# A head's operand loads moved ahead of its predecessor's denominators, and its q and k rows loaded by 6 transfers in place of 12, in a 16-head attention kernel

## The chip, the cores and the metric

The kernel runs on one core of one Trainium2 chip. The metric is the device time of one execution in microseconds (us). Engines are named as in the profile: PE is the matrix engine (PEld its weight loads), DVE the vector engine, ACT the scalar engine, POOL the general-purpose engine, SP the engine that here does nothing but wait on semaphores and start DMA transfers ("SPq" in the profile's rows). Transfers are carried out by 16 DMA engines that the core has.

## The reference

One transformer layer on x of shape (4, 1024, 128), in float32: layer norm, attention with 16 heads of 8 dimensions and a bias that depends only on the distance between query and key, a gate, then a layer norm and a linear layer on values rounded to fp8. The part that matters here:

```python
proj = x @ w_in
k, v, q = jnp.split(proj, 3, axis=-1)          # heads: (b, 16, s, 8)
scores = jnp.einsum('bhqd,bhkd->bhqk', q, k) * scale
scores = scores + _tisa_bias(amplitudes, sharpness, offsets, s)[None]   # a Toeplitz matrix per head
weights = jax.nn.softmax(scores, axis=-1)
attn = jnp.einsum('bhqk,bhkd->bhqd', weights, v)
out = attn.transpose(0, 2, 1, 3).reshape(b, s, d)
gated = out @ w_gate + b_gate
```

## The kernel before, in words

**Setup** (0 to 70 us of the trace): layer norm, the products for q, k and v, and the bias vector of each head. q and k are split in a high and a low float16 part and stored to DRAM (`q_scratch`, `k_scratch`, `store_qk`, line 247); the bias vectors go to `g_scratch` (float32) and to `gh_scratch` and `gl_scratch` (float16 parts).

**Attention** (70 to 563 us) works on one head after another, in a hardware loop of 8 rounds with 2 heads each. A head has 8 groups (`GPH`), one for each 128 keys of every batch entry, and a group has 4 steps, one per batch entry. In a step PE makes 128 x 1024 scores (`scores`, line 869); for three steps of four DVE adds the bias from `t128` and writes them out (`add_bias`, line 938, the instruction is at L945); for the fourth PE adds the bias itself, by a product of `ident2` and `t64`. ACT exponentiates all four (L988, L996), and PE multiplies them with v (`products`, line 899). A ninth column of ones in v makes the softmax denominators, so they fall out of the same products. PE runs two groups ahead of the products with its scores (`LAG` = 2).

**Buffers of a head.** There are two sets: `qb`, `kb`, `t128`, `t64`, used in turn (p = 0, 1). A load fills one set (`load`, line 779): `load_qk` (line 233) brings q rows with 4 transfers and k rows with 8, each row block twice because the high and the low parts are multiplied crosswise; then `load_bias` (1 transfer of 960 KB), `load_bias_parts` (2 of 248 KB) and `load_maxima` (2 small ones). PE waits for all 17 of them before the first score of the head (`head_in`, line 875).

**Denominators of a head.** When the products of a head are complete, DVE and ACT copy them out of PSUM in the second group of the next head (`copy_half`, L736 and L737), and signal `o_ready`. SP then sends the denominators, 4 rows of 1024, to a 128 x 32 tile (`send_denominators`, L765). DVE takes their reciprocals after the additions of the fourth group (`RECIPROCAL` = 3, lines 966 to 975), in its own fixed order. SP stores the reciprocals (L790), waits until they are in DRAM, spreads them back over partitions (L771), waits for the multiplication on POOL (L857, L863), and stores the head's output (L796); that is `normalise_and_store`.

**Order of the work around the change.** Everything is written out by hand. Each engine runs its list in order and stops at a wait. SP's list is the loop from line 815 on. DVE's part of it that matters:

```python
for g in range(2 * GPH):
    for b in range(DPG):
        add_bias(i, g, b)
    ...
    if g == GPH + RECIPROCAL:
        eng.wait_ge(den_in[0], i * 16 + 16)
        eng.reciprocal(dc[0][:, :], dc[0][:, :]).then_inc(inv_ready[0], 1)
```

`z_ready` counts DVE's additions and `sp_ready` the fourth steps that PE has finished, so the two together say that a head's bias and q and k rows have been read for the last time. `groups_done` counts finished groups of products and starts at `SETS` = 4.

Of the kernel before, what the change touches and what calls it, by code (L numbers as in the profile page):

```python
# [22 lines left out]
F16 = mybir.dt.float16  # L23
# [8 lines left out]
H, KB = 16, 21  # L32
HD = D // H
P = 128
NTOK = B * S
# [27 lines left out]
def attention_block(nc, io, out):  # L63
    with ExitStack() as ctx:
# [6 lines left out]
        def dram(name, shape, dt):  # L71
            return nc.dram_tensor(name, shape, dt, kind="Internal").ap()


        q_dram = dram("q_scratch", [2, P, 2, B, HALF], F16)
        k_dram = dram("k_scratch", [2, P, NTOK], F16)
        g_dram = dram("g_scratch", [32, GN], F32)
        gh_dram = dram("gh_scratch", [32, GN], F16)
        gl_dram = dram("gl_scratch", [32, GN], F16)
# [134 lines left out]
        def cols(b):  # L214
            return slice(b * S, (b + 1) * S)
# [16 lines left out]

        def load_qk(eng, h, p, done):

            for c in range(2):
                for rep in range(2):
                    r = ROW * c + 16 * rep
                    eng.dma_start(qb[p][r:r + 16, :],  # L238
                                  q_dram.rearrange("a (h d) c b n -> c h a d (b n)", d=HD)[c, h]).then_inc(done, 16)
            for c in range(2):  # L240
                for hl in range(2):
                    for rep in range(2):
                        r = ROW * c + 16 * hl + 8 * rep
                        eng.dma_start(kb[p][r:r + 8, :],  # L244
                                      k_dram.rearrange("a (h d) n -> h a d n", d=HD)[h, hl]).then_inc(done, 16)

        def store_qk(eng, b, done):

            for ready, part, hl in ((qh_ready, 0, 0), (kh_ready, 2, 0), (ql_ready, 1, 1), (kl_ready, 3, 1)):
                eng.wait_ge(ready, b + 1)  # L250
                src = split[:, part, cols(b)]
                if part < 2:
                    eng.dma_start(q_dram[hl, :, :, b, :], src.rearrange("p (c n) -> p c n", n=HALF))\
                       .then_inc(done, 16)
                else:
                    eng.dma_start(k_dram[hl, :, cols(b)], src).then_inc(done, 16)

        def load_maxima(eng, h, p, done):
            for c in range(2):
                eng.dma_start(qb[p][ROW * c + 32:ROW * c + 33, :],  # L260
                              m_dram[h, :].rearrange("(o b c n) -> c o b n", o=1, c=2, n=HALF)[c]).then_inc(done, 16)
        LOADS = 17
        QK_LOADS = 12
        LOADS_G = 13

        def copy_v(eng, h, p):

# [21 lines left out]
        with nc.Block() as block:  # L289
            @block.sync  # L290
            def _(eng):
# [37 lines left out]
                load_bias(eng, 0, 0, head_in[0])  # L329
                load_bias_parts(eng, 0, 0, head_in[0])  # L330

                for ready, part, dst, rows in ((qh_ready, 0, qb[0], (0, 16)), (ql_ready, 1, qb[0], (8, 24)),
                                               (kh_ready, 2, kb[0], (0, 8)), (kl_ready, 3, kb[0], (16, 24))):
                    eng.wait_ge(ready, B)
                    for c in range(2):
                        src = split[0:HD, part, :]
                        if part < 2:
                            src = src.rearrange("p (b c n) -> p c b n", c=2, n=HALF)[:, c]
                        for r in rows:
                            eng.dma_start(dst[ROW * c + r:ROW * c + r + HD, :], src).then_inc(first_in, 16)  # L340
# [398 lines left out]
        def settled(eng, s, value):  # L739


            eng.wait_ge(s, value)
            eng.sem_inc(queue_steps, 1)
# [30 lines left out]
        with nc.Block() as block:  # L774
            @block.sync
            def _(eng):
                def load(h, p):
                    h = in_range(h)
                    load_qk(eng, h, p, head_in[p])
                    load_bias(eng, h, p, head_in[p])  # L780
                    load_bias_parts(eng, h, p, head_in[p])
                    load_maxima(eng, h, p, head_in[p])
# [29 lines left out]
                eng.sem_inc(queue_steps, 1)  # L812
                with eng.Fori(0, NH2) as i:

                    settled(eng, groups_done, i * (2 * GPH) + SETS)
                    with eng.If(i > 0):
                        settled(eng, o_ready[0], i * 2 + 1)
                        settled(eng, o_ready[1], i * 2 + 1)
                        send_denominators(eng, 1)
                    load(i * 2 + 1, 1)  # L820
                    with eng.If(i > 0):
                        normalise_and_store(i * 2 - 1, 1, i - 1)

                    settled(eng, groups_done, i * (2 * GPH) + (GPH + SETS))
                    settled(eng, o_ready[0], i * 2 + 2)
                    settled(eng, o_ready[1], i * 2 + 2)
                    send_denominators(eng, 0)
                    with eng.If(i < NH2 - 1):
                        load(i * 2 + 2, 0)
                    with eng.If(i > NH2 - 2):  # L830

                        eng.wait_ge(vst_in, H)
                        eng.wait_ge(o_stored[0], 16 * B * NH2)
                        eng.wait_ge(o_stored[1], 16 * B * NH2)
                        for b in range(B):
                            eng.dma_start(num[b][0:EARLY, :], o_dram[b, 0:H - 2]).then_inc(num_in[b], 16)
                    normalise_and_store(i * 2, 0, i)
# [676 lines left out]
```

## Time and profile before

| | us |
|---|---|
| median of 3 runs | 629.25 (627.89 to 629.95) |
| the profiled execution | 628.96 |
| span of its trace | 627.1 |
| PE, DVE, ACT busy | 571.8, 558.1, 551.1 |
| POOL busy | 101.7 |
| DMA traffic | 53.82 MB |

The span is what the trace covers from its first to its last instruction; the 1.9 us between it and the execution's own time lie around it. PE, DVE and ACT are each busy for 88 to 91% of the span. Granted clock of the profiled execution: 0.955 of full speed on average.

### The profile page before, as it was taken

The page shows a single profiled execution, that of the slowest core. Times are in us where ns is not written, and L with a number is a line of the kernel's source. Part 1 is how long each engine was busy: PE and PEld are TensorE (multiplying, and loading weights), DVE is VectorE, ACT ScalarE, POOL GpSimd, SP SyncE. Part 2 cuts the span into 40 slices and gives each one's busy share as a digit, 9 for nine tenths or more (in the row PEclk, how much of TensorE's full clock was granted, in tenths as well). Part 3 has the DMA queues.
Part 4 walks back from the last instruction along what each step waited for, and adds up shares of the span by engine and source line. Part 5 has one row for each costly group of instructions (what it writes and reads, how often), then busy time and mean ns, then how long its engine had stood idle before and what let it go on. Part 6 is the DMA issues. An engine that isn't in the chain of part 4 may idle for free.

```text
span 627.1 us, 12678 instructions
## 1 busy us (share of the span) xinstructions
PE 571.8 (91%) x3987; PEld 155.6 (25%) x3987; DVE 558.1 (89%) x686; ACT 551.1 (88%) x610; POOL 101.7 (16%) x96
## 2 busy tenths in 40 slices
PE   5794399999999999999999899999999999999945
PEld 2442022222222222222222122222222222225532
DVE  6975499999999999999999899999999999974885
ACT  2853399999999999999999999999999999983474
POOL 5731510010101010101010101010101100012630
PEclk8797599999999999999999999999999999999957
DMA  9127642516161616161617161616252434410004
GB/s 234 52 49 194 156 106 45 146 22 137 28 139 26 144 25 142 24 141 29 135 30 133 27 140 37 128 42 126 48 121 65 100 69 96 128 26 9 1 0 135
DMA packets 29819, 53.82 MB, mean 86 GB/s; under 512 B 9461, under 2 KB 20986, under 8 KB 28666
## 3 DMA queue, kind: packets, MB, share of 16 engines
q1 hardware_dynamic: 28954, 53.02, 37.4%
q10 hardware_dynamic: 848, 0.59, 0.3%
q8 instruction: 8, 0.13, 0.1%
q14 instruction: 9, 0.07, 0.0%
HBM read 43.27 MB, written 9.16 MB: 84 GB/s over the span
## 4 chain that ended last, share of the span: by engine, by line
ACT 38%; issue 31%; DVE 7%; DMA 7%; SPq 7%; PE 7%; POOL 1%; ACTq 1%; DVEq 0%; POOLq 0%
ACT pbuf L988 16%; ACT split L988 15%; ACT pbuf L996 3%; DVE pbuf L459 3%; PE ps L1188 3%; ACT split L996 2%; DMA qb<-m_scratch 2%; SPq L340 2%; DMA r_scratch<-dc 2%; PE ps L1232 1%; SPq L238 1%; DMA kb<-split 1%; ACT o_sbs L737 1%; SPq L244 1%; DMA x_sb<-in_L_attn_x 1%
## 5 line engine op out<-in xcount | busy, mean ns | idle before, releaser
L945 DVE TENSOR_TENSOR pbuf<-ps,t 128x1024 f32<-128x1024 f32 x192 | 229.9, 1216 | 21.6 <-PE ps L886 17.5
L945 DVE TENSOR_TENSOR split<-ps,t 128x1024 f32<-128x1024 f32 x192 | 231.3, 1222 | 12.0 <-PE ps L886 6.3
L988 ACT ACTIVATE pbuf<-pbuf 128x1024 f32<-128x1024 f32 x192 | 203.2, 1211 | 21.1 <-DVE pbuf L945 20.9
L886 PE MATMUL ps<-qb,kb 64*128 64x512 f16 x1024 | 183.6, 389 | 23.8 <-SPq L801 15.0
L988 ACT ACTIVATE split<-split 128x1024 f32<-128x1024 f32 x192 | 199.3, 1220 | 0.1
L911 PE MATMUL ps<-split,vst 128*32 128x512 f32 x1024 | 136.0, 604 | 1.0 <-ACT split L996 1.0
L911 PE MATMUL ps<-pbuf,vst 128*32 128x512 f32 x1024 | 136.4, 605 | 0.0
L886 PEld LDWEIGHTS ps<-qb,kb 64*128 64x128 f16 x1024 | 48.5, 92 | 309.6 <-DVE pbuf L945 115.1
L895 PE MATMUL ps<-t64s,ident 128*64 128x512 f16 x512 | 80.1, 393 | 0.0
L996 ACT ACTIVATE split<-ps 128x1024 f32<-128x1024 f32 x64 | 75.7, 1183 | 0.0
L996 ACT ACTIVATE pbuf<-ps 128x1024 f32<-128x1024 f32 x64 | 75.0, 1173 | 0.0
L863 POOL TENSOR_TENSOR o_sbs<-o_sbs,rd 128x1024 f32<-128x1024 f32 x8 | 19.1, 2387 | 196.3 <-DMA rd<-r_scratch 196.3
L857 POOL TENSOR_TENSOR o_sbs<-o_sbs,rd 128x1024 f32<-128x1024 f32 x7 | 16.7, 2385 | 186.0 <-DMA rd<-r_scratch 186.0
L911 PEld LDWEIGHTS ps<-split,vst 128*32 128x32 f32 x1024 | 20.3, 108 | 31.5 <-issue 29.7
L911 PEld LDWEIGHTS ps<-pbuf,vst 128*32 128x32 f32 x1024 | 20.1, 108 | 29.0 <-issue 29.0
L895 PEld LDWEIGHTS ps<-t64s,ident 128*64 128x64 f16 x512 | 18.0, 108 | 31.0 <-issue 31.0
L459 DVE TENSOR_SCALAR pbuf<-x_sb,mv,st 128x128 f32<-128x128 f32 x32 | 18.4, 861 | 1.5 <-POOL st L362 1.5
L1188 PE MATMUL ps<-wgate,v_all 128*128 128x256 f32 x64 | 18.1, 405 | 0.0
L1270 ACT ACTIVATE pbuf<-ps 128x256 f32<-128x256 f32 x16 | 6.0, 381 | 13.3 <-PE ps L1188 13.3
L1122 POOL TENSOR_TENSOR x_sb<-x_sb,pbuf 128x256 f32<-128x256 f32 x16 | 11.5, 725 | 27.8 <-DVE pbuf L1387 27.8
L268 POOL COPY vst<-v_all 128x256 f32 (+1 forms) x16 | 6.4, 398 | 52.1 <-PE ps L911 48.1
L736 DVE COPY o_sbs<-ps 128x512 f32<-128x512 f32 x16 | 10.9, 680 | 3.5 <-PE ps L911 3.5
(144 smaller groups left out, 326.2 us busy)
## 6 DMA issues: line engine op xcount, KB each, us to landing
t<-g_scratch SPq DMA_DIRECT2D x16, 960.0 KB
kb<-k_scratch SPq DMA_DIRECT2D x120, 64.0 KB
t64s<-gh_scratch SPq DMA_DIRECT2D x16, 248.0 KB
t64s<-gl_scratch SPq DMA_DIRECT2D x16, 248.0 KB
qb<-q_scratch SPq DMA_DIRECT2D x60, 64.0 KB
x_sb<-in_L_attn_x SPq DMA_DIRECT2D x4, 512.0 KB, 6.7
q_scratch<-split SPq DMA_DIRECT2D x8, 256.0 KB, 3.3
k_scratch<-split SPq DMA_DIRECT2D x8, 256.0 KB, 3.6
```

Of the source, the lines that this page charges most:

```text
L340: eng.dma_start(dst[ROW * c + r:ROW * c + r + HD, :], src).then_inc(first_in, 16)
L459: last = eng.tensor_scalar(xn[:, n, :], x_sb[:, n, :], mv[:, n, 0:1], st[:, 0, n:n + 1], ALU.subtract, ALU.mult)
L857: eng.tensor_tensor(o_sb[1], o_sb[1], rd[:, :], ALU.mult).then_inc(o_norm, 1)
L863: eng.tensor_tensor(o_sb[0], o_sb[0], rd[:, :], ALU.mult).then_inc(o_norm, 1)
L886: last = eng.matmul(ps[:, u + c, :], kb[p][rows, keys], qb[p][rows, b * HALF:(b + 1) * HALF], start=True, stop=True)
L895: last = eng.matmul(ps[64 * m:64 * m + 64, u + c, :], ident2[:, :], t64[p][:, c0:c0 + HALF], start=False, stop=True, skip_group_check=True)
L911: last = eng.matmul(ps[32 * b:32 * b + 32, 6 + c, :], vst[p][:, b * TB + t, :], slot(g, b)[:, c * HALF:(c + 1) * HALF], start=(t == 0), st ...
L945: eng.tensor_tensor(slot(g, b), banks(unit(k), 2), t128[p][:, t * P:t * P + S], ALU.add).then_inc(z_ready, 1)
L988: eng.activation(buf, buf, ACT.Exp).then_inc(p_ready, 1)
L996: eng.activation(buf, banks(4, 2), ACT.Exp).then_inc(p_ready, 1)
L1122: eng.tensor_tensor(xs, xs, gate[:, j % NG, :], ALU.add).then_inc(x1_ready, 1)
L1188: last = eng.matmul(ps[:, j % 4, m * 2 * D:(m + 1) * 2 * D], num[n // TB][:, (n % TB) * P:(n % TB + 1) * P], wgate[:, :], start=False, sto ...
```

## The change

A head's load no longer waits for the products of the head that used the buffers before. It waits for `z_ready` and `sp_ready`, and stands ahead of `send_denominators` in SP's list, at both places of the loop. `load_qk` brings q rows with 4 transfers and k rows with 2. Each of the six reads its DRAM rows twice by a leading dimension of step 0 and size 2. For that `k_scratch` is laid out by head, and the order of the rows in `qb` and `kb` changes: q is now high, high, low, low and k high, low, high, low, where it was the other way round. The counts of the semaphores follow (11 transfers a head, not 17). The transfers that fill head 0 in the setup keep their number and size.

```diff
-        k_dram = dram("k_scratch", [2, P, NTOK], F16)
+        k_dram = dram("k_scratch", [H, 2, HD, NTOK], F16)
...
         def load_qk(eng, h, p, done):
 
-            for c in range(2):
-                for rep in range(2):
-                    r = ROW * c + 16 * rep
-                    eng.dma_start(qb[p][r:r + 16, :],
-                                  q_dram.rearrange("a (h d) c b n -> c h a d (b n)", d=HD)[c, h]).then_inc(done, 16)
+            def repeated(v):
+                return bass.AP(tensor=v.tensor, offset=v.offset, ap=[[0, 2]] + [list(a) for a in v.ap])
+
             for c in range(2):
                 for hl in range(2):
-                    for rep in range(2):
-                        r = ROW * c + 16 * hl + 8 * rep
-                        eng.dma_start(kb[p][r:r + 8, :],
-                                      k_dram.rearrange("a (h d) n -> h a d n", d=HD)[h, hl]).then_inc(done, 16)
+                    r = ROW * c + 16 * hl
+                    eng.dma_start(qb[p][r:r + 16, :],
+                                  repeated(q_dram.rearrange("a (h d) c b n -> c a h d (b n)", d=HD)[c, hl, h]))\
+                       .then_inc(done, 16)
+            for c in range(2):
+                eng.dma_start(kb[p][ROW * c:ROW * c + 32, :],
+                              repeated(k_dram.rearrange("h a d n -> h (a d) n")[h])).then_inc(done, 16)
...
-        LOADS = 17
-        QK_LOADS = 12
-        LOADS_G = 13
+        LOADS = 11
+        QK_LOADS = 6
+        LOADS_G = 7
...
                 with eng.Fori(0, NH2) as i:
 
-                    settled(eng, groups_done, i * (2 * GPH) + SETS)
                     with eng.If(i > 0):
+                        settled(eng, z_ready, i * (2 * DPH))
+                        settled(eng, sp_ready, i * (2 * GPH))
+                    load(i * 2 + 1, 1)
+                    with eng.If(i > 0):
+                        settled(eng, groups_done, i * (2 * GPH) + SETS)
                         settled(eng, o_ready[0], i * 2 + 1)
                         settled(eng, o_ready[1], i * 2 + 1)
                         send_denominators(eng, 1)
-                    load(i * 2 + 1, 1)
-                    with eng.If(i > 0):
                         normalise_and_store(i * 2 - 1, 1, i - 1)
 
+                    with eng.If(i < NH2 - 1):
+                        settled(eng, z_ready, i * (2 * DPH) + DPH)
+                        settled(eng, sp_ready, i * (2 * GPH) + GPH)
+                        load(i * 2 + 2, 0)
                     settled(eng, groups_done, i * (2 * GPH) + (GPH + SETS))
                     settled(eng, o_ready[0], i * 2 + 2)
                     settled(eng, o_ready[1], i * 2 + 2)
                     send_denominators(eng, 0)
-                    with eng.If(i < NH2 - 1):
-                        load(i * 2 + 2, 0)
```

SP's list at the start of a loop round, before the change. Rows without a tile set registers or branch; sizes are those of the destination.

```order
L816 COMPARE_AND_BRANCH [waits groups_done]
L742 ISA
L765 DMA dc1<-o_sbs 128x1x32 [waits o_ready0,o_ready1]
L816 UNCONDITIONAL_BRANCH
L238 ISA
L238 DMA qb1<-q_scratch 16x1x2048 x2
L238 ISA
L238 DMA qb1<-q_scratch 16x1x2048 x2
L244 DMA kb1<-k_scratch 8x4096 x2
L244 ISA
L244 DMA kb1<-k_scratch 8x4096 x6
```

The same place with the change:

```order
L816 COMPARE_AND_BRANCH
L743 REGISTER_ALU
L743 REGISTER_ALU [waits z_ready]
L816 UNCONDITIONAL_BRANCH [waits sp_ready]
L241 ISA
L241 DMA qb1<-q_scratch 16x1x2048
...
L241 DMA qb1<-q_scratch 16x1x2048
L245 ISA
L245 DMA kb1<-k_scratch 32x1x4096 x2
```

The wait for `groups_done` and `o_ready` and the transfer of the denominators are gone from here, and eight transfers of 8 rows have become two of 32 rows.

SP's list where the load ends, before the change:

```order
L227 DMA t128_1<-g_scratch 128x1920
L230 REGISTER_ALU
L230 DMA t64s<-gh_scratch 64x1984
L231 DMA t64s<-gl_scratch 64x1984
L260 ISA
L260 DMA qb1<-m_scratch 1x4x512
L260 ISA
L260 DMA qb1<-m_scratch 1x4x512
L821 COMPARE_AND_BRANCH
L790 DMA r_scratch<-dc1 128x32 [waits inv_ready1]
```

And with the change:

```order
L227 DMA t128_1<-g_scratch 128x1920
L230 REGISTER_ALU
L230 DMA t64s<-gh_scratch 64x1984
L231 DMA t64s<-gl_scratch 64x1984
L261 ISA
L261 DMA qb1<-m_scratch 1x4x512
L261 ISA
L261 DMA qb1<-m_scratch 1x4x512
L820 COMPARE_AND_BRANCH
L743 ISA
L766 DMA dc1<-o_sbs 128x1x32 [waits groups_done,o_ready0,o_ready1]
L791 DMA r_scratch<-dc1 128x32 [waits inv_ready1]
```

The transfer of the denominators now stands behind all eleven transfers of the load, directly ahead of the one that needs DVE's reciprocals of it.

## Rows read from the trace of the kernel before

**Rows 1.** The page: busy time, then busy tenths of PE in 40 slices.
```profile
PE 571.8 (91%) x3987; PEld 155.6 (25%) x3987; DVE 558.1 (89%) x686; ACT 551.1 (88%) x610; POOL 101.7 (16%) x96
PE   5794399999999999999999899999999999999945
```

**Rows 2.** Waits, 85 to 560 us: total us, times, longest.
```profile
DVE pbuf L945 <- PE ps L886: 2.4, 4, 1.9
PE ps L886 <- DMA qb<-m_scratch: 2.0, 2, 1.8
```

**Rows 3.** Timeline of SP: start us, us, what. One head's sequence, then others.
```profile
110.02 2.97 SPq L238 DMA_DIRECT2D qb<-q_scratch  x4
...
128.23 1.30 SPq L771 DMA_DIRECT2D rd<-r_scratch  x4
...
446.33 0.65 SPq L765 DMA_DIRECT2D dc<-o_sbs  x1
447.22 2.99 SPq L238 DMA_DIRECT2D qb<-q_scratch  x4
450.31 3.06 SPq L244 DMA_DIRECT2D kb<-k_scratch  x8
453.55 0.36 SPq L227 DMA_DIRECT2D t<-g_scratch  x1
...
457.18 0.35 SPq L790 DMA_DIRECT2D r_scratch<-dc  x1
466.83 1.30 SPq L771 DMA_DIRECT2D rd<-r_scratch  x4
473.02 1.81 SPq L796 DMA_DIRECT2D o_scratch<-o_sbs  x4
...
545.83 0.35 SPq L790 DMA_DIRECT2D r_scratch<-dc  x1
547.98 1.28 SPq L771 DMA_DIRECT2D rd<-r_scratch  x4
```

**Rows 4.** Timeline of DVE, the first four groups of the same head.
```profile
438.51 4.96 DVE L945 TENSOR_TENSOR pbuf<-ps,t 128x1024 f32<-128x1024 f32 x4
443.39 0.68 DVE L736 COPY o_sbs<-ps 128x512 f32<-128x512 f32 x1
...
453.93 0.34 DVE L971 RECIPROCAL dc<-dc 128x32 f32<-128x32 f32 x1
```

**Rows 5.** The line that sends denominators: count, durations ns, first and last start us.
```profile
L765 SPq DMA_DIRECT2D dc<-o_sbs x15: 635/641/648, 109.1 to 537.5; - x15
```

**Rows 6.** Windows of 1 us; the last columns are granted clock, DMA share, GB/s.
```profile
450.00:451.00 1.00, 1.00 (x10) 0.16 (x8) 0.76 (x1) 1.00 (x2) 0.00 (x0) 1.00 0.12 49
451.00:452.00 1.00, 1.00 (x14) 0.25 (x10) 1.00 (x2) 1.00 (x2) 0.00 (x0) 1.00 0.60 143
...
458.00:459.00 1.00, 1.00 (x14) 0.24 (x10) 0.99 (x2) 1.00 (x3) 0.00 (x0) 1.00 0.99 240
...
463.00:464.00 1.00, 1.00 (x12) 0.19 (x4) 0.94 (x1) 1.00 (x2) 0.00 (x0) 1.00 0.19 64
464.00:465.00 1.00, 1.00 (x8) 0.24 (x6) 0.96 (x1) 1.00 (x2) 0.00 (x0) 1.00 0.12 47
```

**Rows 7.** Waits of SP over the whole span: total us, times, longest.
```profile
SPq L743 <- DMA r_scratch<-dc: 138.4, 15, 12.0
```

**Rows 8.** Windows around PE's idle stretch in the setup, and the restart after it.
```profile
57.00:60.00 3.00, 0.00 (x0) 0.00 (x0) 0.00 (x0) 0.00 (x0) 0.00 (x0) 0.50 0.51 72
...
73.00:76.00 3.00, 2.83 (x12) 0.39 (x8) 2.50 (x3) 2.85 (x3) 2.88 (x3) 0.50 1.03 350
76.00:79.00 3.00, 2.18 (x18) 0.58 (x18) 3.00 (x3) 2.99 (x4) 2.94 (x2) 0.97 0.82 248
```

**Rows 9.** SP's timeline, the first load of the loop.
```profile
82.12 3.12 SPq L238 DMA_DIRECT2D qb<-q_scratch  x4
```

**Rows 10.** Timeline of all engines where one load came late: idle before, and releaser.
```profile
346.78 0.39 PE L886 MATMUL ps<-qb,kb 64*128 64x512 f16 x2 [1.83 <-DMA qb<-m_scratch]
```

More of the change, by code:

```diff
@@ L255, in store_qk @@
                 else:
-                    eng.dma_start(k_dram[hl, :, cols(b)], src).then_inc(done, 16)
+                    eng.dma_start(k_dram[:, hl, :, cols(b)], src).then_inc(done, 16)
         def load_maxima(eng, h, p, done):
@@ L330, in _ @@
                 load_bias_parts(eng, 0, 0, head_in[0])
-                for ready, part, dst, rows in ((qh_ready, 0, qb[0], (0, 16)), (ql_ready, 1, qb[0], (8, 24)),
-                                               (kh_ready, 2, kb[0], (0, 8)), (kl_ready, 3, kb[0], (16, 24))):
+                for ready, part, dst, rows in ((qh_ready, 0, qb[0], (0, 8)), (ql_ready, 1, qb[0], (16, 24)),
+                                               (kh_ready, 2, kb[0], (0, 16)), (kl_ready, 3, kb[0], (8, 24))):
                     eng.wait_ge(ready, B)
```

## The prediction

> **What bounds the kernel now.** I read the page first, then the waits of the attention stretch, then SP's and DVE's timelines over one head, then the DMA share in windows of 1 us. The page shows PE, DVE and ACT busy at nine tenths or more from slice 6 to slice 38 [rows 1]. No wait of substance stands there: DVE waited 2.4 us in all for PE, and PE 2.0 us in all for a load that was late, 1.8 us of it at one head [rows 2, 10]. So the most that earlier loads can win is about 2 us. The heads follow each other at a steady pace: the denominators are sent 15 times, first at 109.06 (row: 109.1) and last at 537.54 (row: 537.5), so a head takes 428.4 / 14 = 30.6 us [rows 5].
>
> The question is then what the new order can cost. I take one head as the model and count from Z, the end of a head's last addition. In the trace the four additions that begin the next head start at 438.51, so Z = 438.5 [rows 4]. The denominators leave at 446.33, which is Z + 7.8; the load's transfers start at 447.22 [rows 3]; DVE comes to the reciprocal at 453.93, which is Z + 15.4, and finds them there [rows 4]. From the end of the reciprocal to the next Z are 30.6 - 15.4 - 0.3 = 14.9 us of additions that follow it in DVE's list.
>
> **How long a load takes.** Behind the load SP starts the small transfer to `r_scratch` at 457.18 and goes on only at 466.83, when it has landed: 9.65 us for 16 KB [rows 3]. The last such transfer, the only one with no load ahead of it, takes 545.83 to 547.98, 2.15 us [rows 3]. All 15 together cost SP 138.4 us [rows 7]. So a transfer waits for the data of those started before it. From the load's first transfer to that landing are 466.83 - 447.22 = 19.6 us; at an earlier head 128.23 - 110.02 = 18.2 [rows 3].
>
> What sets the 19.6 us? At 450 to 451 only q rows move: the DMA share is 0.12, which is two engines of 16, at 49 GB/s, so 24.5 GB/s each [rows 6]. A q transfer reads 2 x 8 rows, its outermost dimension having size 2. When the k transfers of 8 rows come, the share goes to 0.60; while the bias rows move it is 0.99 at 240 GB/s, 15 GB/s for an engine [rows 6]. At 464 to 465 it is back at 0.12 and 47 GB/s: fourteen engines have finished and two still carry the rest [rows 6]. I read this so: the two engines that carry all q rows are the last to finish, and their bytes set the length of a load.
>
> **The change, part by part.**
>
> 1. *k rows in 2 transfers.* Each reads 256 KB through a source whose outermost dimension is the added one, of size 2, as in the q transfers. I expect two engines again, and the same two, since four q transfers in flight together gave no more than a share of 0.12. Before, each carried an eighth of 8 x 64 KB, 64 KB in all; now half of 512 KB, 256 KB. The extra 192 KB (197,000 B) take 8.0 us at 24.5 GB/s, or 13.1 us at the contended 15 GB/s [rows 6]. I take 8.0, since the other fourteen will long have finished. If the k rows spread as before, it is nothing: the lower end.
>
> [...]
>
> 2. *Six transfers fewer to start.* Eight k transfers take 450.31 to 453.55 on SP, 3.24 us [rows 3]; two at the pace of the q transfers (3.09 us for 4, 0.77 each) take 1.5. That is 1.7 us less. It lets the bias rows start 1.7 us earlier, and I count it in full; at the other end it is worth nothing, where the two engines are never short of work.
>
> So a load and the transfer behind it take 19.6 + 8.0 - 1.7 = 25.9 us.
>
> 3. *Load at Z.* The load now waits for the additions and for PE's fourth step, and starts at Z + 0.5 (0.5 for two waits, a branch and registers: denominators to first q transfer took 0.24 us beyond the first's own 0.65 [rows 3], and there are more of these now). SP must be free by then, see below.
>
> 4. *Denominators behind the load.* They are sent when the load's eleven transfers are started, about Z + 8.5, and land when its data have, at Z + 0.5 + 25.9 = Z + 26.4. DVE reaches the reciprocal at Z + 15.4 and must stop there, because the additions of groups five to eight stand behind it in its list. PE can make only two steps of scores ahead, and ACT gets nothing to exponentiate, so all three stop. The stall is 26.4 + 0.1 - 15.4 = 11.1 us. The cover that the denominators had before (7.6 us between their start and DVE's arrival) is gone.
>
> 5. *Restart.* [...] DVE lost about 1 us there: it was busy 2.50 of 3 us at 73 to 76, and half a us more may be lost before that [rows 8]. I take 1.0; ends 0 and 2.5 (half of 5 us, if PE paced all of it).
>
> Sum of one boundary: 11.1 + 1.0 = 12.1 us; the head takes 42.7 us, not 30.6. SP's other work fits: from the reciprocal at Z + 26.8, 2.2 us to `r_scratch`, then 466.83 to 474.83 for spreading, multiplying and storing, 8.0 us [rows 3], ends by Z + 38, before the next Z at 42.7. And the load has landed long before PE wants it, so the 2.0 us of [rows 2] go.
>
> Heads 0 to 13 have their denominators behind a load, 14 boundaries: 14 x 12.1 = 169.4. Head 1's load starts at 82.12 [rows 9] and now needs until about 107.5, while head 0's Z is 109.1 - 7.8 = 101.3; the load sent at that Z finds the two engines occupied for 4 us longer than it would start itself: + 4. Less the 2.0: 171.4. On the profiled execution's own 628.96 that gives 800.4; that execution lies 0.3 below the median of the runs shown (629.25). I say **800 us**. The layout of `k_scratch` and the new order of the rows change no count of rows or bytes, and the setup's transfers keep their shapes: nothing.
>
> **The rivals.**
>
> *A: the k rows cost no more than before.* If the data spread over engines as they did, a load takes 19.6 - 1.7 = 17.9; or, by the fastest head of [rows 3], 18.2 - 1.7 = 16.5. Denominators land at Z + 18.4: a stall of 3.1, and with a PE that barely cools 0.3 more: 14 x 3.4 - 2 = 46, 675 us. For it: one transfer with 32 destination rows could be cut along those. Against it: q's 16 destination rows did not help q.
>
> [...]
>
> *B: the denominators do not wait (faster or the same).* They are 4 rows, and if they went through engines that are not the two late ones they could land as soon as the bias rows of those have, about 463.3, where the share is down to 0.19 [rows 6], less 1.7 for the earlier start: 14.4 us after the load's first transfer, Z + 14.9. The point that decides is Z + 15.4: below it DVE never stops, the loads are in time, and the 2 us of [rows 2] are won: 627 us. For it: fourteen engines are idle at the end of a load. Against it: the `r_scratch` transfer waited for the last of the load at every head [rows 7], and it would need this margin of 0.5 us at each of 14 heads.
>
> *C: the two engines do worse.* If q and k rows share them at the contended rate throughout, the load takes 19.6 + 13.1 = 32.7, the stall is 17.9 and with 2.5 for the clock a boundary costs 20.4: 629 + 14 x 20.4 + 10 = 925 us. Against it: two engines alone moved 47 to 49 GB/s [rows 6].
>
> **How the numbers follow.** Forecast 0.78; A 0.12; B 0.04; C 0.06. The forecast's own spread comes from the load: the heads of the trace differ by 18.2 to 19.6 and more where a load was late; 22.5 to 29 us for a load make 12.1 into 8.7 to 15.2, so 629 + 14 x 8.7 = 751 to 629 + 14 x 15.2 + 7 = 849. I widen the low side to 740 for k rows that share less evenly. Range 740 to 850. About 0.3% (1.9 us) is what a measurement of this kernel can tell from no change. Faster by more than that 0.02 and within it 0.03 (both from B, and from a load that for some reason is short), slower 0.95.
>
> **What would show it.** In the changed trace DVE's reciprocals (L971 and L975 before) should stand behind an idle stretch of 8 to 14 us whose releaser is the transfer dc<-o_sbs, 14 times; starts of L765's successor about 42.7 us apart; the DMA share in windows of 1 us at 0.12 and some 50 GB/s for 8 us or more at the end of each load; the granted clock down to 0.50 once a head; q and k transfers 4 and 2 a head. Waits of DVE for the denominators under 2 us, or a share near 1 to the load's end, would make it wrong; so would stalls of the size of A with the two-engine tail absent.

## The result and the profile after

The changed kernel takes 782.2 us (median of 4 runs, 778.7 to 784.5) against 629.6: a ratio of 1.242, 95% interval 1.239 to 1.246. It is slower by 153 us. The forecast was 800 with a range of 740 to 850. The profiled execution took 778.7 us, its span is 776.8.

From the page of the changed kernel: busy time, busy tenths of PE in 40 slices, and the granted clock of PE in tenths. They answer to [rows 1].

```profile
PE 599.3 (77%) x3987; PEld 153.8 (20%) x3987; DVE 556.8 (72%) x686; ACT 558.6 (72%) x610; POOL 101.5 (13%) x96
PE   6872978959595968778695959595949687799965
PEclk7795889979798898979797979797978989799976
```

DVE and ACT do the same work as before, within 8 us, and PE is busy longer by 28 us, part of it at the lower clock (0.865 of full speed on average over the execution, 0.955 before). Their share of the span fell because they stand still once a head. The waits of the attention stretch (85 to 710 us) say for what; they answer to [rows 2].

```profile
ACT pbuf L993 <- DVE pbuf L950: 139.7, 43, 9.8
DVE dc L976 <- DMA dc<-o_sbs: 68.4, 7, 10.6
DVE dc L980 <- DMA dc<-o_sbs: 62.5, 7, 10.1
PE ps L891 <- DMA qb<-m_scratch: 5.7, 1, 5.7
```

DVE waited 130.9 us for the denominators in 14 stops: 3.4 us at the first, 9.2 to 10.6 at the others, 9.3 on average. It did not wait for them at all before. ACT waited for DVE in turn.

One head in SP's timeline, as in [rows 3]:

```profile
145.12 3.23 SPq L241 DMA_DIRECT2D qb<-q_scratch  x4
148.55 1.35 SPq L245 DMA_DIRECT2D kb<-k_scratch  x2
...
153.95 0.60 SPq L766 DMA_DIRECT2D dc<-o_sbs  x1
169.86 0.36 SPq L791 DMA_DIRECT2D r_scratch<-dc  x1
...
177.62 1.70 SPq L797 DMA_DIRECT2D o_scratch<-o_sbs  x4
185.89 3.38 SPq L241 DMA_DIRECT2D qb<-q_scratch  x4
```

and the same head in DVE's, as in [rows 4]:

```profile
144.71 4.96 DVE L950 TENSOR_TENSOR pbuf<-ps,t 128x1024 f32<-128x1024 f32 x4
...
169.42 0.35 DVE L976 RECIPROCAL dc<-dc 128x32 f32<-128x32 f32 x1 [9.21 <-DMA dc<-o_sbs]
169.69 3.42 DVE L950 TENSOR_TENSOR pbuf<-ps,t 128x1024 f32<-128x1024 f32 x3
173.60 1.22 DVE L950 TENSOR_TENSOR pbuf<-ps,t 128x1024 f32<-128x1024 f32 x1 [0.50 <-PE ps L891]
175.51 2.54 DVE L950 TENSOR_TENSOR pbuf<-ps,t 128x1024 f32<-128x1024 f32 x2 [0.69 <-PE ps L891]
```

Z is 144.7. The load starts 0.4 us later. The denominators are sent at 153.95, with the load's transfers started, and are there at 169.4: 24.3 us after the load's first transfer, Z + 24.7. Over the 14 heads with a load ahead of their denominators this takes 24.1 to 26.0 us, 24.8 on average. DVE stands from 160.2 on. After the reciprocal it loses 1.2 us more, waiting for PE.

Windows of the same head (the last three columns: granted clock, DMA share, GB/s; the first after the window is PE's busy time), as in [rows 6, 8]:

```profile
153.00:154.00 1.00, 1.00 (x14) 0.24 (x10) 1.00 (x2) 1.00 (x3) 0.00 (x0) 1.00 0.99 379
...
159.00:160.00 1.00, 1.00 (x11) 0.26 (x10) 1.00 (x1) 1.00 (x2) 0.00 (x0) 1.00 0.12 49
...
165.00:166.00 1.00, 0.00 (x0) 0.00 (x0) 0.00 (x0) 0.00 (x0) 0.00 (x0) 0.50 0.11 46
...
171.00:172.00 1.00, 1.00 (x6) 0.23 (x7) 1.00 (x2) 0.94 (x1) 0.00 (x0) 0.50 0.00 0
...
175.00:176.00 1.00, 1.00 (x14) 0.25 (x10) 0.49 (x1) 1.00 (x2) 1.00 (x1) 1.00 0.00 0
```

The share falls from 0.81 at 156 to 157 to 0.18 in the next window: fourteen engines have moved their part of the load by 157. From there to 168, eleven of the 24 us, two engines work alone at 46 to 57 GB/s and a share of 0.11 to 0.18. Two is read from the share (0.12 of 16 engines is 1.9); no view names the engines of a transfer. PE's clock is at half speed, 0.50, from 165 to 174 and back at 1.00 at 175.

The sending of denominators, the row that answers to [rows 5]:

```profile
L766 SPq DMA_DIRECT2D dc<-o_sbs x15: 593/599/612, 118.7 to 687.3; - x15
```

A head takes 568.6 / 14 = 40.6 us, 10.0 more than before (the first of the 14 steps 35.2, the other 13 on average 41.0), and the first denominators leave 9.7 us later. That is 140.1 + 9.7, and the spans differ by 149.7: all of the loss is in these two.

### The profile page after: what moved, and what is told of

It reads as the page before. It is cut to its first block, busy times and chain, and to the rows that moved or that the text cites. A ratio compares the mean times of both kernels' runs of the same rounds, so it can differ in the third digit from the quotient of the medians.

```text
span 776.8 us, 12583 instructions
## 1 busy us (share of the span) xinstructions
PE 599.3 (77%) x3987; PEld 153.8 (20%) x3987; DVE 556.8 (72%) x686; ACT 558.6 (72%) x610; POOL 101.5 (13%) x96
## 4 chain that ended last, share of the span: by engine, by line
DMA 30%; PE 28%; SPq 14%; issue 7%; DVE 6%; ACT 4%; POOL 1%; DVEq 0%; ACTq 0%; POOLq 0%
DMA dc<-o_sbs 28%; PE ps L916 12%; PE ps L891 8%; SPq L241 5%; PE ps L900 4%; DVE pbuf L950 3%; SPq L245 2%; SPq L261 2%; DMA qb<-m_scratch 2%; DVE split L950 2%; PE ps L1193 2%; ACT split L993 1%; SPq L230 1%; ACT pbuf L993 1%; PE ps L1237 1%
## 5 line engine op out<-in xcount | busy, mean ns | idle before, releaser
L993 ACT ACTIVATE pbuf<-pbuf 128x1024 f32<-128x1024 f32 x192 | 197.1, 1059 | 161.9 <-DVE pbuf L950 159.7
L891 PE MATMUL ps<-qb,kb 64*128 64x512 f16 x1024 | 191.8, 409 | 147.3 <-DVE pbuf L950 123.4
L993 ACT ACTIVATE split<-split 128x1024 f32<-128x1024 f32 x192 | 189.4, 1064 | 1.5 <-DVE split L950 1.4
L916 PE MATMUL ps<-split,vst 128*32 128x512 f32 x1024 | 146.0, 646 | 1.0 <-ACT split L1001 1.0
L891 PEld LDWEIGHTS ps<-qb,kb 64*128 64x128 f16 x1024 | 44.3, 94 | 438.3 <-DVE pbuf L950 234.5
L900 PE MATMUL ps<-t64s,ident 128*64 128x512 f16 x512 | 86.3, 420 | 0.0
L1001 ACT ACTIVATE split<-ps 128x1024 f32<-128x1024 f32 x64 | 65.8, 1028 | 0.0
L1001 ACT ACTIVATE pbuf<-ps 128x1024 f32<-128x1024 f32 x64 | 65.1, 1017 | 0.0
L976 DVE RECIPROCAL dc<-dc 128x32 f32<-128x32 f32 x7 | 2.5, 353 | 68.4 <-DMA dc<-o_sbs 68.4
L980 DVE RECIPROCAL dc<-dc 128x32 f32<-128x32 f32 x8 | 2.8, 352 | 62.5 <-DMA dc<-o_sbs 62.5
L916 PEld LDWEIGHTS ps<-split,vst 128*32 128x32 f32 x1024 | 21.0, 112 | 35.2 <-issue 27.6
```

The lines of the kernel that those rows point to most:

```text
L891: last = eng.matmul(ps[:, u + c, :], kb[p][rows, keys], qb[p][rows, b * HALF:(b + 1) * HALF], start=True, stop=True)
L900: last = eng.matmul(ps[64 * m:64 * m + 64, u + c, :], ident2[:, :], t64[p][:, c0:c0 + HALF], start=False, stop=True, skip_group_check=True)
L916: last = eng.matmul(ps[32 * b:32 * b + 32, 6 + c, :], vst[p][:, b * TB + t, :], slot(g, b)[:, c * HALF:(c + 1) * HALF], start=(t == 0), st ...
L993: eng.activation(buf, buf, ACT.Exp).then_inc(p_ready, 1)
L1001: eng.activation(buf, banks(4, 2), ACT.Exp).then_inc(p_ready, 1)
```

## The experiments

Twelve more kernels were run. Z is always the end of a head's last addition; "a head" is the time from one sending of denominators to the next, averaged over the 14 steps of the profiled execution. The length of a load is the time from its first transfer to the landing of the small transfer behind it (denominators or `r_scratch`); the rows show one head, and where a reading rests on the length, the average over 14 heads stands beside it.

| kernel | median, us | ratio to before (95%) | a head, us | DVE's wait for denominators a head |
|---|---|---|---|---|
| before | 628.4 to 629.6 | | 30.6 | 0 |
| the change | 782.2 | 1.239 to 1.246 | 40.6 | 9.3 |
| six transfers, order of before | 696.0 | 1.103 to 1.108 | 34.9 | 0 |
| order of the change, 12 transfers | 721.1 | 1.141 to 1.150 | 36.9 | 5.1 |
| change, denominators on another queue | 668.0 | 1.058 to 1.064 | 32.8 | 0 |
| change, rows interleaved | 630.0 | 1.000 to 1.004 | 30.4 | 0.2 |
| change, reciprocal two groups later | 699.6 | 1.109 to 1.114 | 35.1 | 3.7 |
| interleaved, order of before | 629.8 | 1.000 to 1.003 | 30.5 | 0 |
| interleaved, denominators on another queue | 631.0 | 1.002 to 1.005 | 30.5 | 0.1 |
| before, q by 8 rows | 629.0 | 1.000 to 1.003 | 30.5 | 0 |
| order of the change, q by 8 rows | 708.8 | 1.126 to 1.133 | 36.0 | 4.4 |
| the same, rows spread | 713.2 | 1.130 to 1.138 | 35.9 | 4.8 |
| before, q by 8 rows, rows spread | 629.6 | 1.000 to 1.003 | 30.5 | 0 |
| change, only k's dimensions exchanged | 672.2 | 1.062 to 1.077 | 33.6 | 2.9 |

### One half of the change at a time

**Six transfers, order of before.** The two loop pieces of SP stand as in the kernel before (the `-` lines of the diff's last part), all else as changed.

> The six transfers with the order of before (denominators ahead of the load). Theory (the two engines that carry q and k rows set a load's length, and the order decides who waits for it): the load takes about 24 us from its first transfer as in the changed kernel (145.12 to 169.4), starts at Z + 8.7 and lands at Z + 32.5, where PE wants it at Z + 29.1; no wait of DVE for denominators, but PE waits about 3.4 us a head for the load, 14 x 3.4 and some 5 us at head 1: 680 us (665 to 695). Rival (the k rows cost nothing, the order alone costs): 627 to 630 us.

Measured 696.0 us. The wait over 85 to 640 us, and the row of the line that sends the denominators:

```profile
PE ps L887 <- DMA qb<-m_scratch: 48.3, 15, 6.2
```
```profile
L766 SPq DMA_DIRECT2D dc<-o_sbs x15: 624/635/654, 120.6 to 609.7; - x15
```

No wait of DVE for denominators; PE waits for the load at every head, 42 us at 14 of them and 6.2 at head 1: 3.0 a head against 3.4 expected. The mechanism is as foretold. The time is 16 us over the 680 and 1 us above the range, because each stop costs 1.3 us beyond its own length (a head is 4.3 us longer) and the start loses 11.5 us, not 5. So the six transfers alone make the kernel slower.

**Order of the change, 12 transfers.** The kernel before with SP's two loop pieces from the change.

> The order of the change with the 12 q and k transfers of before. Theory: the denominators still land with the load's data, 19.6 us (18.2 to 22.5) after its first transfer, at Z + 20.1 against DVE's arrival at Z + 15.4: DVE stops for 4.7 us a head, with restart 5.3, so 14 x 5.3 - 2 = 72 us more: 701 us (680 to 720). Rival (only the bytes on two engines are at fault and an early load is good by itself): 627 to 630 us.

Measured 721.1 us, 1 us above the range expected. SP's timeline:

```profile
474.53 3.02 SPq L238 DMA_DIRECT2D qb<-q_scratch  x4
...
495.21 0.35 SPq L790 DMA_DIRECT2D r_scratch<-dc  x1
```

The load and what is behind it take 20.3 us (474.53 to 494.9, with 0.35 for the reciprocal taken off). DVE waits 5.1 us a head and a head grows by 6.3. So the new order is harmful with the old transfers too. The two halves alone cost 68 and 93 us, the whole change 153.

### Who holds the denominators back

**Denominators on another queue.** In the changed kernel POOL sends them, behind its `copy_v`:

```diff
@@ SP @@
-                        settled(eng, o_ready[0], i * 2 + 1)
-                        settled(eng, o_ready[1], i * 2 + 1)
-                        send_denominators(eng, 1)
@@ POOL @@
                     with eng.If(i > 0):
+                        settled(eng, o_ready[0], i * 2 + 1)
+                        settled(eng, o_ready[1], i * 2 + 1)
+                        send_denominators(eng, 1)
                         settled(eng, rd_in, i * (2 * 16 * B))
```

and the same for the other buffer.

> The changed kernel, but the denominators are sent by POOL, on its own queue, as soon as they are ready. Theory (a transfer waits for those started before it in its own queue, not for busy engines): they land within 3 us of their start, DVE's waits of 131 us for dc<-o_sbs go to under 10 us. What is left is SP's own cycle: load 24.2 us to its landing, then 8 us of spreading, multiplying and storing, 0.5 to the next load: 32.7 us a head, 2.1 above 30.6, so about 660 us (640 to 675). Rival (any small transfer waits while the two engines are occupied): no change, 775 to 790 us.

Measured 668.0 us, a head 32.8 us where 32.7 was worked out. The denominators' row and SP's timeline:

```profile
L766 POOL DMA_DIRECT2D dc<-o_sbs x15: 693/693/930, 118.8 to 577.6; - x15
```
```profile
452.13 0.36 SPq L791 DMA_DIRECT2D r_scratch<-dc  x1
467.13 1.30 SPq L772 DMA_DIRECT2D rd<-r_scratch  x4
```

The load still takes 24 us (443.0 to 467.1 here), but DVE waits 0.4 us in the whole execution. This late head does not test the queue, though: SP is behind by then, its load starts at 443.0, and POOL sends the denominators at 444.2, when the load has hardly begun. The second head does test it. Its rows from the timelines of SP, POOL and DVE:

```profile
141.59 3.25 SPq L241 DMA_DIRECT2D qb<-q_scratch  x4
...
149.25 0.70 POOL L766 DMA_DIRECT2D dc<-o_sbs  x1 [1.45 <-ACT o_sbs L738]
...
156.58 0.34 DVE L976 RECIPROCAL dc<-dc 128x32 f32<-128x32 f32 x1
...
165.78 1.30 SPq L772 DMA_DIRECT2D rd<-r_scratch  x4
```

All transfers of the load are started when POOL sends the denominators, DVE takes them without a stop 15.0 us after the load's first transfer, and the load lands at 24.2 us. So the denominators need not wait for the load once they are out of SP's queue. That it is the queue and not the engines is not shown: no row here tells which DMA engines carry a transfer that POOL sends, and they may be others than those of SP's. Nor is the way quite free. At the third head the denominators took 7.9 us to land, against 3.4 in the median of all.

The next thing in SP's queue, the store to `r_scratch`, now waits in their place, 15 us, and with it SP's cycle of load, spreading and storing. So the loads come late and PE waits for them, 12 times and 28.6 us in all. That the head came out at the 32.7 us worked out is partly luck: the first three steps take 30.5 us, the other eleven 33.4.

**Reciprocal later.** One constant, `RECIPROCAL = 5` in place of 3.

> The changed kernel with the reciprocal two groups later in DVE's list (RECIPROCAL 5, not 3). Theory (DVE stops only for what is left of the load when it arrives): DVE arrives at Z + 22.9, the denominators land at Z + 24.7 if SP starts the load at Z. But SP's storing now ends 9.9 us after the reciprocal, at Z + 33.2, 2.5 us after the next Z, so the load starts and lands 2.5 us later: a stall of 3.9 us a head (9.3 before), with restart 4.3, 14 x 4.3 + 6 = 66 us above the kernel before: 694 us (675 to 710). Rival (the time goes with the later start of anything behind the load, whatever DVE does): within 10 us of the changed kernel's 782.

Measured 699.6 us; DVE waits 52.1 us in all (the row: total, times), 3.7 a head against 3.9 expected:

```profile
  DMA dc<-o_sbs: 52.1, 13
```

DVE's fixed place for the reciprocal is the point that decides, as the prediction used it. SP's cycle takes back part of what a later place wins: at the head whose Z is 213.9 the load starts only at 216.7.

### What makes the load long

**Rows interleaved.** The same six transfers and bytes, but each source begins with its rows. For k the doubling moves inside. For q the inner dimension is now the high and the low part, and each of the two transfers brings both once. q and k rows are put in the order that fits, in the setup too.

```diff
             def repeated(v):
-                return bass.AP(tensor=v.tensor, offset=v.offset, ap=[[0, 2]] + [list(a) for a in v.ap])
+                rows, row = [list(a) for a in v.ap]
+                return bass.AP(tensor=v.tensor, offset=v.offset, ap=[rows, [0, 2], row])
...
-                for hl in range(2):
-                    r = ROW * c + 16 * hl
+                for a in range(2):
+                    r = ROW * c + 16 * a
                     eng.dma_start(qb[p][r:r + 16, :],
-                                  repeated(q_dram.rearrange("a (h d) c b n -> c a h d (b n)", d=HD)[c, hl, h]))\
+                                  q_dram.rearrange("a (h d) c b n -> c h d a (b n)", d=HD)[c, h])\
                        .then_inc(done, 16)
```

> The changed kernel with the same 6 transfers and the same bytes, but the rows interleaved, so that the source's outermost dimension has size 16 for k (each row doubled in the second dimension) and 8 for q. Theory (the outermost dimension sets the number of engines): no stretch at a DMA share of 0.12, a load lands about 14 to 15 us after its first transfer, the denominators at Z + 15 to 16, DVE stops for 0 to 1 us a head: 632 us (625 to 650). Rival (the doubled reading itself is slow, or the engines are chosen otherwise): as the changed kernel, 750 to 790 us.

Measured 630.0 us, 152 us less than the change; what differs is the order of the source's dimensions and the order of the rows that goes with it.

SP's timeline, then windows of 1 us as above:

```profile
442.38 3.27 SPq L242 DMA_DIRECT2D qb<-q_scratch  x4
...
458.08 0.36 SPq L792 DMA_DIRECT2D r_scratch<-dc  x1
```
```profile
452.00:453.00 1.00, 0.71 (x6) 0.24 (x6) 1.00 (x2) 1.00 (x2) 0.00 (x0) 1.00 1.18 353
...
456.00:457.00 1.00, 1.00 (x10) 0.32 (x8) 0.91 (x2) 1.00 (x2) 0.00 (x0) 1.00 0.14 24
```

The denominators are there 15.3 us after the load's first transfer (no head has them later than 15.9), and the load ends without the tail of two engines that took eleven us in the change: from 454 to 457 the share goes 0.76, 0.39, 0.14, and then it is 0.00.

**Only k's dimensions exchanged.** The changed kernel, with the k source as above and q as it is.

> The changed kernel with the two dimensions of the k source exchanged: 16 rows outermost, the doubling inside. The q transfers stay as they are. Heads 1 to 15 then multiply k rows with other q rows than they should, so the attention's values differ; the work is the same. Theory (each term by itself: k's 192 KB on the two engines made the load long, q's 128 KB on them are left): the load takes 16.5 to 18 us and not 24.2, the denominators land at Z + 17 to 18.5 against Z + 15.4, DVE stops for 1.5 to 3 us a head: 655 us (640 to 675). Rival (the doubled read or the size of 256 KB is at fault, not the dimension's place): 770 to 790 us.

Measured 672.2 us. SP's timeline, and the total and number of DVE's waits for the denominators:

```profile
472.20 3.21 SPq L241 DMA_DIRECT2D qb<-q_scratch  x4
...
490.57 0.36 SPq L793 DMA_DIRECT2D r_scratch<-dc  x1
```
```profile
  DMA dc<-o_sbs: 40.5, 14
```

The load takes 17.9 us (17.8 on average) and DVE waits 2.9 a head, both inside what was expected. So of the 24.3 us, 6.4 are k's bytes on two engines (7.0 on the averages), and that alone is 110 of the 153 us lost; the rest goes when q's dimensions are exchanged too (15.3 us to the landing, above).

### Are the two engines all of it?

In the kernel before, by the prediction's reading, q's two-engine transfers set the load's length. **q by 8 rows** tests it:

```diff
-                    r = ROW * c + 16 * rep
-                    eng.dma_start(qb[p][r:r + 16, :],
-                                  q_dram.rearrange("a (h d) c b n -> c h a d (b n)", d=HD)[c, h]).then_inc(done, 16)
+                    for hl in range(2):
+                        r = ROW * c + 16 * rep + 8 * hl
+                        eng.dma_start(qb[p][r:r + 8, :],
+                                      q_dram.rearrange("a (h d) c b n -> c h a d (b n)", d=HD)[c, h, hl]).then_inc(done, 16)
```

> The kernel before with one thing changed: each q transfer of 2 x 8 rows is split into two of 8 rows, 16 q and k transfers a head; order, setup stores and row order of before. Theory (q's two-engine transfers set the load's length in the kernel before too): the load to the landing behind it takes about 15 us instead of 19.6, the tail at a DMA share of 0.12 is gone, PE's 2.0 us of waits for loads go, nothing else changes: 627 us (625 to 629), at best 0.3% below before. Rival: four transfers more cost as much as they win, 629 us or more.

Measured 629.0 us, not to be told from before, and the reason given was wrong for the most part. The landing hardly moved (SP's timeline, then windows):

```profile
446.55 3.19 SPq L239 DMA_DIRECT2D qb<-q_scratch  x8
...
466.28 1.30 SPq L772 DMA_DIRECT2D rd<-r_scratch  x4
```
```profile
456.00:457.00 1.00, 1.00 (x10) 0.26 (x8) 0.94 (x2) 1.00 (x2) 0.00 (x0) 1.00 1.18 127
457.00:458.00 1.00, 1.00 (x10) 0.16 (x8) 1.00 (x2) 1.00 (x2) 0.00 (x0) 1.00 0.86 92
```

It comes 19.7 us after the first transfer, where the model head of the kernel before had 19.6. Over 14 heads the averages are 19.6 here and 20.5 before, so doing without the two engines was worth about 1 us. The tail of two engines is gone (the share is 0.56 at 463 to 464, 0.38 at 464 to 465, then 0.00), but for some four us in the middle, 455 to 459, the engines are busy at a share of 0.84 to 1.20 and move only 92 to 127 GB/s, where the kernel before had 240 at a share of 0.99 [rows 6].

**The same in the new order.**

> The same 8-row transfers with the early load of the change and the denominators behind it. Theory: the load is short again, so the denominators land at about Z + 15 to 16 against DVE's Z + 15.4, DVE stops for 0 to 1 us a head: 630 us (626 to 640), as with interleaved rows. The number of transfers (20 here, 11 in the change) does not matter. Rival (the number of transfers ahead of the denominators matters): 20 transfers start over about 10 us, so the denominators leave 2 to 3 us later than with 11 and 650 us or more result.

Measured 708.8 us: this expectation failed. A load was not short (19.5 us on average), and DVE waited 62.0 us in all, 4.4 a head. The rival's bound of 650 us was passed, but not for its reason: in the head traced the denominators left 10.1 us after the load's first transfer, where they left after 8.8 in the change, and landed 9.7 us after that. Transfers of eight rows, without a two-engine one among them, are not enough. What the runs show is the slow stretch, 92 to 127 GB/s at a share of 0.84 to 1.20 in the kernel before with q by 8 rows. That it comes from writing each transfer's rows to eight neighbouring partitions was a guess of mine, which no run shows; theory P below is that guess, and the numbers of engines named with theory E are assumed too. **Rows spread** sends the same transfers to every fourth of 32 partitions (`kb[p][r:r + 29:4, :]` for `kb[p][r:r + 8, :]`, likewise for `qb`, with the row order made to fit).

> The kernel with the early load and 8-row transfers that gave 708.8 us, with one thing changed: the 8 rows of a q or k transfer go to every fourth partition, over 32, and not to 8 adjacent ones. Same number of transfers, same bytes, same engines. Theory P (many engines that write into few neighbouring partitions hold each other up, and the bias rows behind them in the same queues): the load becomes as short as with interleaved rows, about 15 us, and the time 630 us (626 to 640). Theory E (what counts is that k rows use 8 engines and not 16, or that there are 20 transfers): no change, 700 to 715 us.

Measured 713.2 us, which is what theory E said, but the trace shows that the test did not isolate what it was to isolate:

```profile
470.86 6.25 SPq L239 DMA_DIRECT2D qb<-q_scratch  x8
...
487.13 0.61 SPq L766 DMA_DIRECT2D dc<-o_sbs  x1
490.95 0.34 SPq L791 DMA_DIRECT2D r_scratch<-dc  x1
```

A transfer to stepped partitions took SP 0.78 us to start, not 0.40, so the load's transfers needed 15.8 us and the denominators were sent 16.3 us after the first; they landed 3.4 us later. Here SP's starting is most of the landing's 19.7 us. **The same with the order of before:**

> The same spread rows with the order of before (denominators first). Theory P: the landing behind a load comes 15 us after its first transfer and not 19.7; PE waits for no load; 628 us (626 to 630), since there are only about 2 us to win. Theory E: 19.7 us to the landing and 628 to 630 us; the time does not tell them apart here, the landing does.

Measured 629.6 us, and the landing 19.9 us after the first transfer. By its own rule that would speak for theory E, but this test has the same fault as the one before it:

```profile
447.52 6.24 SPq L239 DMA_DIRECT2D qb<-q_scratch  x8
...
463.68 0.35 SPq L791 DMA_DIRECT2D r_scratch<-dc  x1
467.39 1.30 SPq L772 DMA_DIRECT2D rd<-r_scratch  x4
```

SP needed 16.2 us of the 19.9 to start what stands ahead of the small transfer. The landing decides between the theories as little as the time does. The row of the bias phase:

```profile
462.00:463.00 1.00, 1.00 (x10) 0.10 (x2) 1.00 (x2) 1.00 (x2) 0.00 (x0) 1.00 1.12 453
```

At the same DMA share as the slow stretch above the engines now move 453 GB/s. That fits theory P, but in this kernel the k rows were over before the bias rows began, so it does not prove it. The place of the rows, the overlap with the bias rows and the number of engines stay unseparated.

### Is there anything to win?

**Interleaved, order of before.** The interleaved kernel with SP's loop as before.

> Interleaved rows in 6 transfers, order of before (denominators ahead of the load). Theory: a load lands about 15 us after its first transfer instead of 19.6, so PE never waits for it (2.0 us in the kernel before) and DVE never for denominators (2.8 us in the interleaved kernel with the early load): 626 us, 2 below before (624 to 628.5). Rival (fuller use of the engines slows the three busy engines in another way): 630 us or more.

Measured 629.8 us, ratio 1.0003 to 1.0027, above the 624 to 628.5 expected. The load takes 13.5 us at this head, the shortest of 14; the average is 15.5, near the 15 expected:

```profile
447.67 3.22 SPq L242 DMA_DIRECT2D qb<-q_scratch  x4
...
461.15 1.30 SPq L773 DMA_DIRECT2D rd<-r_scratch  x4
```

PE no longer waits for a load, and a head takes 30.5 us, 1.8 less over 14 heads as forecast. But in its trace the first denominators leave at 111.5, 2.4 us later than in the profile of before, and the end is no earlier. Part of that may be chance: the kernel before with q by 8 rows has the setup of before, and its first leave at 110.4. Part is in the setup (a store to the new layout of `k_scratch` takes SP 0.6 us, not 0.35, in two places; its first scores start at 72.1, not 70.8); the shares were not separated.

**Interleaved, denominators on another queue.**

> Interleaved rows, the early load of the change, and denominators sent by POOL on its own queue. Theory: no engine waits for a load or for denominators; SP's cycle (load 15, then 8 to 10 of storing) is below 30.6 us: 626 us (624 to 628.5), equal to the interleaved kernel in the order of before. Rival (an early load or POOL's own sending costs something by itself): 2 us or more above that.

Measured 631.0 us, 1.002 to 1.005. DVE waits 0.8 us in all and PE for no load, and the time is no better; the 626 us expected of both kernels did not come. The trace is of the fastest of its 12 executions (629.0 us; the slowest took 634.0), so it does not show what the median has beyond it. No version beat the kernel before. Of the versions with the order of the change, only those with interleaved rows came within 0.5% of it.

## Why the prediction was right

The forecast's mechanism is what happened, and the time was 18 us below the 800, inside the range. The profiled execution grew by 149.7 us where the sum has 171.4. Its stops were shorter (130.9 us in all, not 155.4) and its restarts cheaper (9.2, not 14), while the start cost more (9.7, not 4), and the 2.0 taken off at the end are already in the head's 40.6. Step by step:

*What bounds it, and the 2 us to win.* Right. The kernels without any late load gained those 2 us in the loop and no more.

*A transfer waits for those ahead of it.* Right for the denominators in SP's queue, at every head of the changed kernel: they landed 24.1 to 26.0 us after the load's first transfer. Denominators that POOL sent in the middle of a load did not wait for its end (15.0 us against 24.2 at the second head), so the rule is not one for any small transfer; whether queue or engines make the difference stayed open.

*Part 1, k rows on two engines, 8.0 us.* The mechanism is shown: two engines alone, at a share of 0.12, and 6.4 us of load length by exchanging k's dimensions alone (24.3 to 17.9 us). The place of one dimension decides here; rival A fell. The size is not: see part 2. The 192 KB behind the 8.0 take it that k's eight-row transfers ran on eight engines, these two among them. No run shows that number: the share was 0.60 when the k rows came [rows 6], and 0.30 to 0.31 while q moved by 8 rows (447 to 450, in the kernel before with q by 8 rows). What the runs show in the term's place is the 6.4 us (7.0 on the averages).

*Part 2 and the length of a load, 25.9.* Measured 24.3 at the head shown, 24.8 on average. This is the term that was mis-sized. Parts 1 and 2 together add 6.3 us (8.0 - 1.7) to a load; from the average of the kernel before, 20.5, to that of the change it was 4.3. The model head's 19.6 lies below that average (18.2 to 22.5), so the forecast came closer than its reasoning: the low base hid part of the error, by luck. The sum added k's bytes to the 19.6 us of before as if nothing else in them changed. But the 19.6 seems to have held a cost that left with the old k transfers: behind their 8-row pieces the engines moved 240 GB/s at a share of 0.99 [rows 6], and with k on two engines up to 379 at the same share. That this is why is my estimate from the windows, not tested by itself. The reading that the two engines set the 19.6 in the kernel before was wrong for the most part: without them it was 19.7 at one head, and on average 19.6 against 20.5.

*Part 3, load at Z.* Z + 0.4 against Z + 0.5; SP was free at 179.3, well before the next load.

*Part 4, DVE's stop.* 11.1 forecast, 9.8 measured on average at 13 heads, 3.4 at the first, which came late for another reason (below). The 1.3 us at the 13 are part 2's shorter load and a little of part 3. So 13 stops, not 14, lay in the 8 to 14 us named as the sign.

*Part 5, restart 1.0.* A head grew by 10.0 us with a wait of 9.3, so 0.7 on average. In the other kernels with stops it was 0.1 to 1.3. The clock fell to 0.50 and came back, as forecast. The upper end of 2.5 took 5 us of work at half clock, as in the setup, where PE worked again from 70.8 and had 0.50 until 76 [rows 8]. At the head shown it was about 3: PE worked again from 170.9, and the clock was 0.50 until 174, 0.59 from 174 to 175 and 1.00 after.

*The one-off terms.* I had + 4 for the first heads; the start is 9.7 us later. 5.7 of it is PE's wait for head 1's load, which I had moved into the next stop rather than counted by itself. 2.2 came before: head 0's additions end at 103.7, not 101.5, 1.3 of it because DVE waits 1.8 us, not 0.5, for a store to `k_scratch`. The forecast had put the new layout at nothing. The rest, about 2, is DVE waiting for PE after its restart. Partly that is returned: the first step after it, 118.7 to 153.95, takes 35.2 us and not 40.6, since DVE came late to that reciprocal too.

*Rivals.* B fell: the denominators landed no earlier than 24.1 us after the load's first transfer at any of 14 heads. C fell: the load did not come near 32.7 us, and the two engines kept 46 to 57 GB/s while alone.

## What to carry to other kernels

Before a load is moved ahead of a small transfer in a queue, ask who waits for the small one: here 16 KB that DVE wanted 15 us after Z stood behind 2.3 MB that PE wanted 29 us after it. Merging transfers is not by itself a gain (696.0 us with the six transfers alone, 628.4 to 629.6 before): look at the outermost dimension of the source, since here a load took 24.3 us with 2 there for k and 17.9 with 16, and look for a DMA share near the 0.12 measured here at the end of a load. When an old duration is used as the base of a sum, ask which of its parts go away with the change.

## What was not expected of the hardware

With eight-row transfers to eight neighbouring partitions there were stretches with all engines busy at a share of 1.18 and only 127 GB/s, where the bias rows alone, after spread rows, moved 453 GB/s at 1.12. The cause is not settled.

Starting a transfer of 8 rows to every fourth partition took SP 0.78 us, to adjacent ones 0.40 (6.24 and 3.19 us for eight).

PE's clock fell to 0.50 also where PE stood still only from 455 to about 457.6. With k's dimensions exchanged DVE waited 3.3 us at that head, and windows of 1 us show it (PE's busy time first, the clock third from the end). At the 1.8 us of [rows 10] in the kernel before it had not fallen: it is 1.00 in every window from 343 to 349.

```profile
455.00:456.00 1.00, 0.00 (x0) 0.00 (x0) 0.00 (x0) 0.07 (x1) 0.00 (x0) 1.00 0.03 4
...
457.00:458.00 1.00, 0.38 (x2) 0.19 (x4) 1.00 (x2) 0.41 (x1) 0.00 (x0) 0.64 0.11 16
458.00:459.00 1.00, 1.00 (x6) 0.18 (x4) 1.00 (x2) 0.93 (x2) 0.00 (x0) 0.50 0.01 4
```
